# Cross pairs' rows of maxima on quarters of TensorE's rows, four products at once, with the rows of maxima standing twice

## The reference, cut to what matters

```
q = (xq @ Wq).reshape(B, N, 16, 64); k, v likewise from xc
scores = einsum('bnhd,bshd->bhns', q, k) * 64 ** -0.5
attn = softmax(scores, axis=-1)              # self: S = 512, cross: S = 154
out = einsum('bhns,bshd->bnhd', attn, v).reshape(B, N, 1024) @ Wo + bo
```

## Time and profile before

| | |
|---|---|
| median of three executions | 459.01 us (456.38 to 459.06) |
| the profiled execution | 459.38 us, span 457.5 us, mean granted clock 0.996 |
| PE busy | 440.9 us, 96% |
| DVE, ACT, POOL busy | 281.0, 240.7 and 218.8 us |

### The profile page before, as it was taken

One profiled execution on the slowest core, in us unless ns is written; L12 is line 12 of the kernel. 1 busy time (PEld: TensorE's weight loads), 2 busy tenths in 40 slices (PEclk: granted clock), 3 DMA queues, 4 the chain that ended last, 5 costly groups with the idle time before them and its releaser, 6 DMA issues.

```text
span 457.5 us, 7065 instructions
## 1 busy us (share of the span) xinstructions
PE 440.9 (96%) x2772; PEld 264.9 (58%) x2772; DVE 281.0 (61%) x513; ACT 240.7 (53%) x326; POOL 218.8 (48%) x190
## 2 busy tenths in 40 slices
PE   7999999989999999999999999999999999999896
PEld 3654664566555656655555855444575554853796
DVE  1766737576875584658756668348736677362753
ACT  2855555555557265665545446455516664257432
POOL 5388101038884796544546656854218333264010
PEclk9999999999999999999999999999999999999899
DMA  8600000000000100000001100020010000000000
GB/s 257 207 1 2 1 1 0 1 0 1 1 0 2 34 1 0 1 0 1 1 1 46 34 4 0 2 69 1 0 47 1 1 2 1 1 0 1 0 20 28
DMA packets 7984, 8.89 MB, mean 19 GB/s; under 512 B 560, under 2 KB 6128, under 8 KB 7952
## 3 DMA queue, kind: packets, MB, share of 16 engines
q1 hardware_dynamic: 7952, 8.45, 6.1%
HBM read 7.92 MB, written 0.52 MB: 18 GB/s over the span
## 4 chain that ended last, share of the span: by engine, by line
PE 86%; DVE 7%; ACT 4%; issue 2%; DMA 1%; SPq 0%
PE PV L797 18%; PE ST L766 14%; PE M L739 7%; PE ST L366 5%; PE ST L768 5%; PE M L845 5%; PE ST L705 5%; PE DEN L812 3%; PE M L887 2%; ACT PT L1387 2%; PE ST L721 2%; PE ST L708 2%; PE ST L378 1%; DVE maxw L1592 1%; PE ST L710 1%
## 5 line engine op out<-in xcount | busy, mean ns | idle before, releaser
L1226 POOL TENSOR_TENSOR psums<-PT 128x1024 f32<-128x1024 f32 (+1 forms) x32 | 76.2, 2382 | 129.6 <-ACT PT L1387 129.5
L1387 ACT ACTIVATE PT<-ST 128x1024 f32<-128x1024 f32 (+1 forms) x96 | 98.0, 1025 | 39.6 <-PE ST L768 38.0
L766 PE MATMUL ST<-R 64*128 64x512 f32 (+1 forms) x576 | 104.9, 406 | 0.4 <-DVE R L1727 0.4
L1740 DVE TENSOR_REDUCE maxw<-M 128x1 f32<-128x512 f32 x128 | 83.6, 687 | 33.7 <-PE M L739 33.3
L797 PE MATMUL PV<-PT,V 128*64 128x512 f32 (+1 forms) x384 | 89.7, 601 | 0.0
L1230 POOL TENSOR_TENSOR psums<-psums,PT 128x1024 f32<-128x1024 f32 x32 | 76.4, 2388 | 2.5
L739 PE MATMUL M<-R 64*128 64x512 f32 (+1 forms) x256 | 71.5, 360 | 1.4 <-DVE maxw L1740 0.8
L766 PEld LDWEIGHTS ST<-R 64*128 64x128 f32 (+1 forms) x576 | 57.5, 171 | 15.1 <-ACT PT L1387 8.0
L739 PEld LDWEIGHTS M<-R 64*128 64x128 f32 x256 | 37.1, 184 | 37.1 <-issue 26.0
L797 PEld LDWEIGHTS PV<-PT,V 128*64 128x64 f32 (+1 forms) x384 | 24.6, 136 | 53.7 <-issue 51.0
L1395 ACT ACTIVATE AT<-PV 128x512 f32<-128x512 f32 x32 | 19.1, 598 | 59.7 <-PE PV L797 59.7
(11 more groups left out here) (267 smaller groups left out, 685.8 us busy)
## 6 DMA issues: line engine op xcount, KB each, us to landing
Wo<-in_wo SPq DMA_DIRECT2D x2, 512.0 KB, 6.5
xnT<-in_xT SPq DMA_DIRECT2D x2, 256.0 KB, 3.5
psums<-in_sel SPq DMA_DIRECT2D x1, 512.0 KB, 4.5
X<-in_x SPq DMA_DIRECT2D x1, 512.0 KB, 5.8
w<-in_w SPq DMA_DIRECT2D x2, 256.0 KB, 6.2
PT<-in_wq SPq DMA_DIRECT2D x1, 512.0 KB, 7.1
PT<-in_wk SPq DMA_DIRECT2D x1, 512.0 KB, 7.3
PT<-in_wv SPq DMA_DIRECT2D x1, 512.0 KB, 7.9
```

Source lines behind the costliest of these rows:

```text
L766: return pe.matmul(u[0:ph.KC, h, :], R[head(h), g % 3, part_k, 1, k], R[head(h), g % 3, part_q, 0, :], start=(n == 0), stop=False)
L1226: ins = pool.tensor_tensor(s, p[:, 0], p[:, 1], ALU.add)
L1387: act.activation(PT1[0:ph.KC, g % 2, c], bank(("st", g, c))[0:ph.KC, :, :], ACT.Exp, scale=HD ** -0.5).then_inc(ph.exp, 1)
L1740: ins = dve.tensor_reduce(maxw[:, g % 2, 0, at:at + 1], m[:, :], AX, ALU.max, negate=True)
```

## The change

The transpose in `turn_pair` becomes four plain fp32 products. Each takes 32 columns of `maxw` as its stationary block and the identity as what moves, and writes 32 of the 128 output rows. The first two take the 32 columns of head 0, the last two those of head 1, so that each head's rows of maxima stand twice. This is so for all 32 pairs. The columns lie 8 apart (before 16), and a head's all lie in 32.

Self pairs keep their product with 64 rows, which now sums both copies, each times 0.5. Cross pairs no longer have one product per chunk and head. Behind chunk 0's scores four products follow, one for each chunk and head, each with 32 rows of its own and into a PSUM bank of its own; those of chunk 1 open its sums, and chunk 1's scores are added behind them. The tile of chunk 1 is therefore claimed ahead of all four. A factor of 2 in `maxima_rows` makes up for the 0.5, with one instruction as before.

```diff
-                pe.transpose(u[:, 0:P], maxw[:, g % 2, 0, :], ident[:, :]).then_inc(t_full, 1)
+                for r in range(4):
+                    k = HD * (r // 2)
+                    ins = pe.matmul(u[32 * r:32 * r + 32, 0:P], maxw[:, g % 2, 0, k:k + 32], ident[:, :], start=True, stop=True)
+                    ins.then_inc(t_full, 1)
...
-                u = claim(("st", g, c), ph.exp, ph.units * i + c + 1)
+                cross = ph is cross_att
+                if not cross or c == 0:
+                    claim(("st", g, c), ph.exp, ph.units * i + c + 1)
+                u = bank(("st", g, c))
...
-                                         start=(n == 0), stop=False)
+                                         start=(n == 0 and not (cross and c == 1)), stop=(n == 2 and cross and c == 1))
...
-                for n in range(5 if unit is not None else 4):
+                last = 2 if cross else 3
+                for n in range(last + 1 + (unit is not None)):
...
-                        if part == 3:
+                        if part == last and not (cross and c == 0):
                             ins.then_inc(ph.st, 1)
+                if cross and c == 0:
+                    pe.wait_ge(mrow_set, g + 1)
+                    second = claim(("st", g, 1), ph.exp, ph.units * i + 2)
+                    for d, dst in enumerate((u, second)):
+                        for h in range(2):
+                            r = slice(HD * h + 32 * d, HD * h + 32 * d + 32)
+                            ins = pe.matmul(dst[0:ph.KC, h, :], onesr[r, 0:ph.KC], mrows[r, g % 2, :],
+                                            start=(d == 1), stop=(d == 0))
+                            if d == 0:
+                                ins.then_inc(ph.st, 1)
...
-                        at = HD * h + 16 * c
+                        at = HD * h + 8 * c
...
-                        at = HD * h + 32 * c
-                        ins = dve.tensor_reduce(maxw[:, g % 2, 0, at:at + 32:16],
+                        at = HD * h + 16 * c
+                        ins = dve.tensor_reduce(maxw[:, g % 2, 0, at:at + 16:8],
...
-                dve.wait_ge(t_full, g + 1)
+                dve.wait_ge(t_full, 4 * (g + 1))
...
+                if g < NPAIR:
+                    ins = dve.tensor_tensor(dst, turned, mask, ALU.mult)
+                else:
+                    ins = dve.scalar_tensor_tensor(dst, turned, 2.0, mask, ALU.mult, ALU.mult)
+                ins.then_inc(mrow_set, 1)
...
-        cols[16 * q::HD, COL["tile"] + q] = 1
-    cols[::16, COL["ones"]] = 1
+        cols[8 * q::32, COL["tile"] + q] = 1
+    cols[::8, COL["ones"]] = 0.5
```

More of the change, by code:

```diff
@@ L1752, in maxima_rows @@
                     dve.wait_ge(old.st, 2 * old.units * (o + 1))
[L1753 to L1756, removed]
+                dst = mrows[:, g % 2, :].rearrange("p (t n) -> p t n", t=TB)
+                turned = half_bank(("turn", g))[:, 0:P].unsqueeze(1).to_broadcast([P, TB, P])
+                mask = cols[:, COL["tile"]:COL["tile"] + TB].unsqueeze(2).to_broadcast([P, TB, P])
+                if g < NPAIR:
[3 more added lines that the diff above has]
+                ins.then_inc(mrow_set, 1)
             def inverse(k):
```

## The result

The changed kernel takes 468.86 us (median of 4, 468.37 to 469.96), against 457.88 us for the kernel before in the same comparison. The ratio is 1.0245, with an interval of 1.0217 to 1.0274, so it is 11.2 us slower (9.9 to 12.5). I had said 472 us, within 464 to 477, from a profiled execution of 459.4 us: +12.8.

What follows compares the result with a forecast made beforehand. PE was taken to bound the kernel, busy 440.9 of 457.5 us. The profiled 459.4 us plus 10.2 for the turn and 2.6 for the cross pairs gave 472.2, stated as 472 us, range 464 to 477.

Steps and rivals of the forecast that it cites:

- PE is the bound, pieces count in full: Attention loop: PE busy 440.9 of 457.5 us, so its time counts in full unless PE waits for something independent.
- The turn, 0.35 us: All 32 pairs: four plain products take 0.35 us, +0.24 over the transpose; with effects on following work, +10.2 us.
- The prices behind it: Behind the turn: full-shape work 0.20 us longer in 18 pairs, two absorbing 0.12; L812 saves 0.12; elsewhere nothing.
- The cross pairs, + 0.17 us each: Rows of maxima in 16 cross pairs: four quarter-row products add 0.17 us in 15 of them, +2.6 us.
- the removed round: Round behind chunk 1's scores, 0.23 us on PE: wins nothing, since L705 then waits longer for chunk 0's exponential.
- the change back: Array division changed back behind the four quarter-row products: 0.20 us, costing nothing within the 0.23 us a removed round leaves.
- the first change: Change from half to quarter rows ahead of the four products: delays chunk 0's exponential, 0.17 us, between 0.15 and 0.20.
- The last pair, 0: Rows of maxima in the last pair: VectorE wait hides one division change, the other replaces the removed round: 0.
- Half of each change hides: Rival: weights load under cover, so a change of array shape costs some 0.10 us or less; 465 us, chance 0.13.
- The removed rounds win: Rival: each cross-pair round comes off and the turn lasts no longer than the transpose: -3.7 us, 455.7 us, chance 0.05.
- Not side by side: Rival: the turn's four products run one after another, 0.22 us each: 20 us more, 492 us, chance 0.05.
- The claim waits: Rival: chunk 1's tile comes late in four pairs behind a spread, a few tenths each, 1 us; no chance given.

Runs made afterwards that it cites:

- only-turn kernel: Changed kernel with only the turn's four plain products kept; cross pairs add rows of maxima by halves, one round per chunk, as before: 467.25 us, ratio 1.0216.
- plain-product kernel: Against the kernel with one full transpose and four quarter-row products: the turn is one full-width plain fp32 product instead: 463.67 us, ratio 1.0134 to before.
- two kernels without maxima: Kernel before with cross pairs' rows of maxima left out: chunk 1's only, 455.77 us (ratio 0.9977); both chunks', 452.79 us (ratio 0.9924).
- kernel by halves: Changed kernel with the old transpose; cross pairs' four products in the new place, but by halves of the rows in two rounds: 456.91 us, ratio 0.9995.
- one transpose: Changed kernel with the turn as one full transpose, VectorE copying each head's columns once more, four quarter-row products kept: 460.11 us, ratio 1.0062 to before.

## Why the prediction was right

**PE is the bound, pieces count in full.** Right: pieces added on PE came through, in the only-turn kernel 9.9 us of the 10.2 forecast.

**The turn, 0.35 us.** Right: 0.36, from a row of the same form with a quarter of the columns. The prices behind it held too: full-shape work + 0.19 (0.20 forecast), + 0.07 where it had waited (0.08), L812 - 0.13 or 0.14 (0.12), nothing ahead of L797. By these rows 31 x 0.25 + 16 x 0.19 + 2 x 0.07 - 5 x 0.13 = 10.3 us. That is a little high, in part since four of the 16 (L527 and L545) grew by 0.15 only. From the start of the first turn to the start of the output products the only-turn kernel's trace has 347.65 us and that of the kernel before 337.63, so the turn costs 10.0.

A plain fp32 record costs what a transpose costs, 0.11 us, and a plain product two of them: the plain-product kernel shows 0.22 us, a factor of 2. The Trainium skill (TensorE: Matmul & The Clock Gate, Terms) calls the transpose mode "4× faster for FP32". The trace does not agree, and the measurement decides.

**The cross pairs, + 0.17 us each.** The mechanism was right for most pairs: the removed round is given back in the wait for chunk 0's exponential (shown by the two kernels without maxima), the change back costs nothing because it lies in that wait, and what counts is the first change. From L739 to the end of the rows of maxima a pair took 1.33 us (307.28 to 308.61), and now 1.51 (313.30 to 314.81), + 0.18. But from there to the turn it was 2.36 us (308.61 to 310.97), and is 2.32: the 0.03 us of waiting that I left as it was has been won back. So it is 0.14 in this pair.

Two things in the other pairs were not in the prediction. In g = 19, 20, 27 and 28 L705 waits for chunk 1's exponential, and it did so before; in the changed kernel in g = 19:

```profile
329.72 1.03 ACT PT L1405
```

There the removed round is a gain, but both changes of shape stand ahead of that exponential. From the end of the first L739 piece to the end of the last product ahead of it, it was 320.57 to 322.67, 2.10 us, and is 327.47 to 329.70, 2.23. That the cost comes out at 0.13 here as well is a coincidence of sizes, not the path that I had named. And in g = 22 the claim waits, as the kernel by halves shows: the pair takes 0.41 us more than with the turn alone (7.30 against 6.89), where the prediction had said that the claim costs nothing. The other 13 of the pairs 16 to 29 take 0.12 to 0.18 more. Whole traces, from the first turn to the output products, differ by 2.1 us between the only-turn kernel (347.65) and the changed one (349.77), forecast 2.6.

**The last pair, 0.** Mis-sized by 0.2 us. Its turn starts at 411.68 before and at 424.03 after, by the timelines:

```profile
411.68 0.27 PE L752 MATMUL M<-ident,maxw 128*128 128x128 f32 x1
```

```profile
424.03 0.42 PE L754 MATMUL M<-ident,maxw 128*32 128x128 f32 x8
```

The last scores end at 417.24 before, and after the change at 429.38:

```profile
428.06 0.46 PE ST L797 x4
428.52 0.85 PE ST L773 x6
```

That is 5.56 and 5.35 us. The turn's 0.25 was covered as forecast, and 0.2 was won besides. From the start of the rows of maxima on the chain has 1.31 us instead of 1.39, since here no exponential holds the saved round and it outweighs the change back. The other 0.1 lies ahead of them: before, PE waited for VectorE's rows, which ended at 415.81, 4.13 us behind the turn's start; now the chain goes over PE's own scores (L773), which end at 428.04, 4.01 us behind it.

**The sum.** 10.0 + 2.1 = 12.1 us at the same clock, the last pair included, forecast 12.8. The spans differ by 10.6, because the profiled execution before lost 1.6 to the clock. In the compared runs it is 11.2 (9.9 to 12.5). The forecast was added to a profiled execution with the lower clock, at 459.4 us, and the changed kernel ran without it, so a part of the 3 us by which 472 is too high is the clock and no term of the sum.

**The rivals.** *Half of each change hides*: no place shows half; the nearest are L527 and L545 behind a turn, 0.15 instead of 0.20. *The removed rounds win*: the four products do run side by side, but the changes of shape on both sides and the exponential take the gain. The Trainium skill (TensorE: Matmul & The Clock Gate, Part 3) gives 3.07x for four such products. The trace agrees in that all four lie within 0.46 us where one lasts 0.45; the factor itself no run here measures. *Not side by side*: excluded by the timeline. *The claim waits*: it does, but in one pair and not in the four behind a spread, for 0.4 us in all, inside the range.

## What to carry to other kernels

Dividing the array more finely pays only for a run of products; for a single round count the change of division on both sides (here 0.13 to 0.20 us each, nearly the 0.23 of a whole round of 512 columns) and look whether one of its neighbours already has that shape. Before counting a removed instruction as gain, follow the next wait behind it: here ACT's exponential, started ahead of the removed round, held PE to the same time. Follow it in every kind of pair: where a spread stood in between, another exponential was the one waited for, and where products were moved up behind an earlier claim, one pair in sixteen had to wait for it. And a transpose is not to be swapped for plain fp32 products as if they cost the same.

## What the runs showed of the hardware

The modelled durations hide a change of shape: the quarter products' records are only 0.05 us longer than the half ones (0.448 against 0.393), and the price stands in the gap ahead of them, in which no weights are loaded (0.41 us). A lower granted clock came in three of the nine profiled executions (before, one transpose, chunk 1's rows left out), each time at the same 64 short products in a row: they took 8.66, 8.74 and 8.37 us, and 7.14 or 7.15 in the other six. What brings it is not shown: just ahead of it PE was busy 17.56 of 19 us before and 17.46 of 19 in the changed kernel, which passed the place at the full clock.
